# Transposing the probabilities of an attention block in two row tiles of 64 queries

## The reference, cut to what matters

```python
# x: (8, 512, 32, 32); 1024 positions per image, 8 heads of 64 channels
xs = layernorm_over_channels(x).reshape(8, 512, 1024).transpose(0, 2, 1)
q, k, v = (xs @ W.T + b for each of the three)          # (8, 8 heads, 1024, 64)
attn = softmax(q @ k.T / 8, axis=-1)                     # (8, 8, 1024, 1024)
x = x + reshape(attn @ v) @ Wo.T + bo
# then a second part on tokens: layer norm, two small three-layer nets on a few
# decoded inputs per token, and a few output channels that they add to
```

## Time and profile before

| | us |
|---|---|
| median of 3 runs | 2739.97 (2738.19 to 2744.03) |
| profiled execution, device time | 2740.56 |
| its span, first to last instruction | 2738.8 |
| TensorE busy with matmuls | 2551.9 (93%) |
| VectorE busy | 1912.3 (70%) |
| ScalarE busy | 1725.9 (63%) |
| GpSimd busy | 895.9 (33%) |
| mean share of TensorE's clock that was granted | 0.974 |

### The profile page before, as it was taken

One profiled execution on the slowest core, in us unless ns is written; L12 is line 12 of the kernel. 1 busy time (PEld: TensorE's weight loads), 2 busy tenths in 40 slices (PEclk: granted clock), 3 DMA queues, 4 the chain that ended last, 5 costly groups with the idle time before them and its releaser, 6 DMA issues.

```text
span 2738.8 us, 37216 instructions
## 1 busy us (share of the span) xinstructions
PE 2551.9 (93%) x13344; PEld 2084.1 (76%) x13344; DVE 1912.3 (70%) x3507; ACT 1725.9 (63%) x3048; POOL 895.9 (33%) x804
## 2 busy tenths in 40 slices
PE   4999999999899998999999999899999999989986
PEld 4788767887688776887778877788777887778864
DVE  4677657776577865778657776677766777667763
ACT  3677547774477744778357773577646775467742
POOL 0244313443134330443314433144412444024430
PEclk9999999999999999999999999999999999999997
DMA  6223203331123311223112240222302323122310
GB/s 244 62 74 100 105 16 89 81 124 62 31 76 82 121 62 46 78 74 127 47 62 74 74 141 22 69 72 73 141 16 73 81 66 135 31 77 74 88 40 31
DMA packets 79941, 215.14 MB, mean 79 GB/s; under 512 B 9968, under 2 KB 10256, under 8 KB 74000
## 3 DMA queue, kind: packets, MB, share of 16 engines
q1 hardware_dynamic: 79760, 212.77, 25.8%
HBM read 103.68 MB, written 25.17 MB: 47 GB/s over the span
## 4 chain that ended last, share of the span: by engine, by line
PE 79%; DVE 12%; ACT 6%; issue 1%; DMA 0%; POOL 0%; SPq 0%; ACTq 0%; DVEq 0%
PE pT L482 14%; PE pJ L446 10%; PE pO L495 9%; PE pO L496 8%; PE pS L467 7%; PE pS L468 7%; PE pa L547 6%; PE po L619 5%; PE pv L446 4%; PE pv L594 3%; ACT PH L707 2%; DVE PL L825 1%; DVE nmax L796 1%; PE pa L656 1%; ACT PR L676 1%
## 5 line engine op out<-in xcount | busy, mean ns | idle before, releaser
L404 POOL TENSOR_SCALAR PR<-PR,rinv 128x1024 f32<-128x1024 f32 x512 | 575.4, 1124 | 1335.1 <-DVE rinv L800 1335.1
L825 DVE TENSOR_TENSOR PL<-pT,PH 128x512 fp32r<-128x512 f32 x1024 | 658.7, 684 | 323.3 <-ACT PH L707 321.5
L707 ACT ACTIVATE PH<-pT 128x512 fp32r<-128x512 f32 x1024 | 557.6, 596 | 370.3 <-PE pT L482 358.4
L796 DVE TENSOR_REDUCE nmax<-pS 128x1 f32<-128x1024 f32 x512 | 621.9, 1216 | 47.7 <-PE pS L468 39.6
L676 ACT ACTIVATE PR<-pS,nmax 128x1024 f32<-128x1024 f32 x512 | 573.1, 1119 | 8.7 <-DVE nmax L796 5.7
L482 PEld LDWEIGHTS pT<-ident,PR 128*128 128x128 f32 x4096 | 479.0, 141 | 109.6 <-POOL PR L404 30.7
L482 PE MATMUL pT<-ident,PR 128*128 128x128 f32 x4096 | 538.1, 274 | 23.6 <-DVE KHL L306 11.6
L467 PE MATMUL pS<-KHL,QS 128*128 128x512 f32 x1024 | 418.2, 408 | 4.6 <-ACT PR L676 2.2
L495 PE MATMUL pO<-PH,VS 128*128 128x512 f32 x1024 | 410.3, 401 | 8.3 <-DVE OT L816 8.3
L496 PE MATMUL pO<-PL,VS 128*128 128x512 f32 x1024 | 406.7, 397 | 0.0
L468 PE MATMUL pS<-KHL,QS 128*128 128x512 f32 x1024 | 404.6, 395 | 0.0
(11 more groups left out here) (143 smaller groups left out, 3176.0 us busy)
## 6 DMA issues: line engine op xcount, KB each, us to landing
KHL<-HL SPq DMA_DIRECT2D x192, 256.0 KB, 3.6
X<-in_x SPq DMA_DIRECT2D x64, 512.0 KB, 6.4
WQ<-wqk_split SPq DMA_DIRECT2D x64, 512.0 KB, 4.2
QS<-HL SPq DMA_DIRECT2D x192, 128.0 KB, 3.0
WO<-wo_split SPq DMA_DIRECT2D x16, 1024.0 KB, 7.3
out<-X SPq DMA_DIRECT2D x16, 1024.0 KB, 4.2
KHL<-wv_split SPq DMA_DIRECT2D x14, 1024.0 KB, 8.9
KHL<-KHL SPq DMA_DIRECT2D x16, 512.0 KB, 4.2
```

The costliest lines, as they stand in the source:

```text
L404: pool.tensor_scalar(PR[g % 2][:, :], PR[g % 2][:, :], M["rinv"][:, g:g + 1], 1.0, ALU.mult, ALU.mult)\
L707: act.activation(PH[ck % 2][:, 4 * half:4 * half + 4, (g % 4) * P:(g % 4 + 1) * P], pT[half][:, :].rearrange("p (k n) -> p k n", k=4), ACT ...
L796: dve.tensor_reduce(nmax[:, g:g + 1], pS[g % 2][:, :], AX.X, ALU.max, negate=True).then_inc(S["a_max"], 1)
L825: dve.tensor_tensor(PL[ck % 2][:, ks, qs], pT[half][:, :].rearrange("p (k n) -> p k n", k=4), f32(PH[ck % 2][:, ks, qs]), ALU.subtract).th ...
```

## The change

Each block of 128 queries x 128 keys is transposed as two blocks of 64 queries, on partitions 0 to 63 and 64 to 127 of `PR`, each with a 64 x 64 part of the identity. The two alternate. Queries 0 to 63 go to `pT[0]` for all eight key blocks and queries 64 to 127 to `pT[1]`. The copies of ACT and DVE take the same number of elements in other slices. The waits for `a_lo` are merged into one ahead of the whole turn.

```diff
     def turn(i, g):
         wait("a_norm", i, g + 1)
-        for half in range(2):
-            if g >= 1:
-                wait("a_lo", i, 2 * (g - 1) + half + 1)
-            elif half == 1:
-                wait("f_qk_lo", i, 4)
-            elif i > 0:
+        if g >= 1:
+            wait("a_lo", i, 2 * g)
+        else:
+            wait("f_qk_lo", i, 4)
+            if i > 0:
                 wait("b_yf", i - 1, 4)
-            for k in range(4):
-                kb = 4 * half + k
-                mm = pe.transpose(pT[half][:, k * P:(k + 1) * P], PR[g % 2][:, kb * P:(kb + 1) * P], ident[:, :])
-            mm.then_inc(S["a_tr"], 1)
+        for kb in range(ST):
+            for half in range(2):
+                rows = slice(half * D, (half + 1) * D)
+                mm = pe.transpose(pT[half][:, kb * D:(kb + 1) * D], PR[g % 2][rows, kb * P:(kb + 1) * P], ident[rows, rows])
+                if kb == ST - 1:
+                    mm.then_inc(S["a_tr"], 1)
...
             for half in range(2):
                 wait("a_tr", i, 2 * g + half + 1)
-                act.activation(PH[ck % 2][:, 4 * half:4 * half + 4, (g % 4) * P:(g % 4 + 1) * P],
-                               pT[half][:, :].rearrange("p (k n) -> p k n", k=4), ACT.Copy).then_inc(S["a_hi"], 1)
+                qs = slice((g % 4) * P + half * D, (g % 4) * P + (half + 1) * D)
+                act.activation(PH[ck % 2][:, :, qs], pT[half][:, :].rearrange("p (k n) -> p k n", k=ST), ACT.Copy)\
+                   .then_inc(S["a_hi"], 1)
...
             for half in range(2):
-                ks = slice(4 * half, 4 * half + 4)
-                qs = slice((g % 4) * P, (g % 4 + 1) * P)
+                qs = slice((g % 4) * P + half * D, (g % 4) * P + (half + 1) * D)
                 wait("a_hi", i, 2 * g + half + 1)
-                dve.tensor_tensor(PL[ck % 2][:, ks, qs], pT[half][:, :].rearrange("p (k n) -> p k n", k=4),
-                                  f32(PH[ck % 2][:, ks, qs]), ALU.subtract).then_inc(S["a_lo"], 1)
+                dve.tensor_tensor(PL[ck % 2][:, :, qs], pT[half][:, :].rearrange("p (k n) -> p k n", k=ST),
+                                  f32(PH[ck % 2][:, :, qs]), ALU.subtract).then_inc(S["a_lo"], 1)
```

## The result

| | before | after |
|---|---|---|
| median | 2741.81 us (4 runs) | 2787.53 us (4 runs, 2784.31 to 2790.22) |
| ratio | | 1.0168, 95% interval 1.0152 to 1.0185 |
| profiled execution, device time | 2740.56 | 2784.31 |
| its span | 2738.8 | 2782.5 |
| granted share of TensorE's clock | 0.974 | 0.970 |

The kernel before has one run more here than in the table ahead of the prediction. The change costs 1.7%. The forecast was 3014 us, 10% more; the rival "the tiles run at once, the drains stay" gave 2775 us and is the case that came.

What follows compares the result with a forecast made beforehand. The prediction took TensorE to bound the kernel. To 2740.56 us it added 227 for costlier turns and 46 for the merged wait, giving 3014 us, 10% slower, with a range of 2765 to 3100.

Steps and rivals of the forecast that it cites:

- the tiles run at once, the drains stay: Rival for the turns: 0.83 us each, -20 us, but the loop loses 54 us, so 2775 us; chance 0.20.
- What bounds the kernel: Whole kernel: TensorE bounds it, on 79% of the chain and busy 211.62 of 217.00 us in an image's attention steps.
- the loop beside it: Turn, ACT's copies, DVE's remainders, next turn: DVE ends 2.61 us after the turn's start; at present costs next to nothing.
- The transposes themselves: In each turn: sixteen pairs at 0.062 us take 0.99 us, 0.12 more than now.
- The load's price by its columns: In the transposes: a skill rule gives 107 ns per 128-column load, a turn of 1.71 us; set aside for L648's 0.062.
- In and out of 64-row tiles: At each turn's borders: changing row count drains TensorE, 0.33 us more per turn.
- The halves end together, and the wait is one: In short steps: ACT starts 0.60 us later, next turn waits for both remainders; 5.8 us per image, 46 us in all.
- the term of 227: TensorE's turns: 0.12 + 0.33 = 0.45 us more each, over 504 turns, 227 us.
- ACT's and DVE's copies at nothing: Copies in runs of 64: same elements, nothing to 5 ns more, on the loop only, 0 us.
- The sum: Whole kernel: 2740.56 us + 227 + 46 = 3013.6, given as 3014 us, 10% slower.

Runs made afterwards that it cites:

- run 3: The changed kernel with its sixteen transposes reordered, all eight of rows 0 to 63, then all eight of rows 64 to 127: 2891.23 us (1.0535).
- run 1: The kernel before with one extra 64-row, 64-column transpose ahead of each turn: 2917.23 us (1.0634).
- 4: The kernel before, 128-row transposes, with only the merged wait for `a_lo` ahead of each turn: 2784.32 us (1.0155).
- 5: The kernel before, 128-row transposes, with the merged wait and both `a_tr` signals at the end of the turn: 2866.20 us (1.0445).

## Why the prediction was wrong

- **What bounds the kernel**: right. TensorE sets the cycle, and the loop beside it was where the prediction put it, 2.61 us long to DVE's end.
- **The transposes themselves: the step that failed.** "I take 0.062 per pair: 16 x 0.062 = 0.99 us" priced sixteen pairs one after the other. The price of 0.062 holds (run 3), but within one tile; two tiles run side by side. From first to last start the forecast has 15 x 0.062 = 0.93 us and the trace 0.49 (0.76 before): 0.44 x 504 = 222 us. The forecast's term of 0.12 us more per turn was a saving. The first couple stands 0.11 us ahead of the second, so that even the rival's 0.50 for a whole turn, its last slot included, was 0.05 short. L648 was the nearest row in columns, but it has only one tile, and no row of before could show two. The rule of the Trainium skill that the prediction quoted (TensorE: Matmul & The Clock Gate, Part 3) agrees with the trace after: it says some 4 ns between tiles, and the couples start 4 ns apart. The evidence for one tile at a time was an absence of rows, and a chance of 0.20 for the rule was too low.
- **The load's price by its columns.** The other rule of the Trainium skill weighed there (TensorE: Matmul & The Clock Gate, LDWEIGHTS), by which the prediction had 107 ns for 128 columns, was rightly set aside: in one tile the pairs with 128 stationary columns are 0.062 us apart.
- **In and out of 64-row tiles**: right in kind. Predicted 0.33 us per turn; 0.28 between transposes (run 1 less a slot of 0.06), 0.24 in the changed kernel in place of the old borders. The rule of the Trainium skill (TensorEngine Tiling (Array Packing), Key Properties) that a change of tiling mode drains the engine agrees with the trace: the first 64-row transpose of a turn starts 0.32 us after the matmul before it, where a stream has 0.23.
- **The halves end together, and the wait is one**: right in kind, and it alone decides the sign: of the forecast's 273 us the term of 227 turned into some 20 us of gain, and this one, put at 46, stayed. The short step was put at 3.27, or 2.84 in the rival; 2.87 was measured. Two errors nearly cancel there: from DVE's end to the first transpose it is 0.15 us, not 0.06, but ACT starts 0.80 us after the turn, not 0.87. In the rival that came the loss was put at 54 us; the idle time ahead of L482 grew by 62. The short steps lost what was foretold, 28 us of waits against 30; the late ones 36 against 23, since their waits for DVE took the place of those for POOL.
- **ACT's and DVE's copies at nothing**: right, 596 and 685 ns.
- **The sum**: with the failed term replaced, the rival's -20 + 54 gives 2775 us for the profiled execution, which took 2784.31. Most of what is missing is the 8 us of idle time just named.

The seven edges, from the turn of step 63 to that of step 1 of the next image by the starts of L482, take 875.3 us before, 878.2 with the wait alone and 881.8 after, so 6.5 of the 43.7 us arise there. In the same stretches the clock was granted at half for 84, 99 and 117 us; from step 11 to step 63 it was granted in full throughout, in all three. How much of the 6.5 us is the merged wait of step 0 and how much the clock was not separated. Whether both tiles could write one bank, so that the first half of the key blocks ends early as before, was not tried; run 3 shows that the two tiles don't keep the order of the program.

## What to carry to other kernels

Before an engine's work is made shorter, measure the loop that its result goes round through the other engines; a new form that ends later, or that waits for everything at once, moves that loop ahead of the engine, and then the shortest step pays, not the mean. Here the wait alone cost 43 us, and even work per step gave 54 back, 16 of which it gives without the wait too. Use a tiled form only in the steps with more work than the loop is long.

A change of the row count costs at both ends, going in and coming out, so two row tiles pay only if the stream between the borders shrinks by more than the 0.24 to 0.28 us measured here.

## What the runs showed of the hardware

- Two 64-row transposes in different row tiles start 3 to 4 ns apart, loads and matmuls both, or alternate 0.031 us apart; in each tile the next follows after 0.062 us. One tile alone goes at 0.062 per pair with 64 as with 8 moving columns.
- TensorE doesn't need them interleaved: with eight of one tile ahead of eight of the other, it starts the second tile's when three of the first are left, against the order of the program, and the turn streams in 0.79 us instead of 0.93.
- A single 64-row transpose among 128-row ones costs 0.34 us, a 128-row one 0.11.
- From the end of a DVE instruction to the start of the transpose that waits for it, it is 0.146 to 0.148 us in the short steps of four kernels (the changed one, runs 3, 4 and 5).
- The granted clock was at its half level only in the edges, at the ends of the program and in the first ten steps of an image, in every kernel here. In the changed kernel it stayed at the full one from step 11 to step 63, though transposes waited 0.35 to 1.0 us there.
